# The clip of the new q and the seeds of stage 0: one VectorE operation over two PSUM banks in place of two

## The reference, cut to what matters

```python
def _derivative(q, p, drive, coupling, bias):
    i_couple = jnp.tanh(q) @ coupling.T
    dq = q - q ** 3 / 3.0 - p + drive + i_couple + bias
    dp = EPSILON * (q + ALPHA - BETA * p)
...
q_next = q + DT / 6.0 * (dq1 + 2 * dq2 + 2 * dq3 + dq4)
q_next = jnp.clip(q_next, -CLAMP, CLAMP)
```

## Time and profile before

| | |
|---|---|
| median of 3 runs | 619.08 us (618.81 to 619.54) |
| profiled execution, its own time | 620.08 us |
| its span | 618.2 us |
| granted TensorE clock, mean | 0.997 |
| PE busy | 582.3 us, 94% |
| DVE busy | 518.4 us, 84% |
| ACT busy | 407.9 us, 66% |
| POOL busy | 255.7 us, 41% |

### The profile page before, as it was taken

One profiled execution on the slowest core, in us unless ns is written; L12 is line 12 of the kernel. 1 busy time (PEld: TensorE's weight loads), 2 busy tenths in 40 slices (PEclk: granted clock), 3 DMA queues, 4 the chain that ended last, 5 costly groups with the idle time before them and its releaser, 6 DMA issues.

```text
span 618.2 us, 14209 instructions
## 1 busy us (share of the span) xinstructions
PE 582.3 (94%) x4918; PEld 525.3 (85%) x4918; DVE 518.4 (84%) x1544; ACT 407.9 (66%) x968; POOL 255.7 (41%) x401
## 2 busy tenths in 40 slices
PE   8899999999999889988888999999999999999997
PEld 7899999999999878877776887887887888888875
DVE  3777777777777768888988999999999999999996
ACT  2544454545454465567447888888888889888885
POOL 0333333332322453420154455565565565565550
PEclk9999999999999999989999999999999999999999
DMA  8400000000000000500000000000000000000001
GB/s 270 165 2 2 1 1 2 1 1 2 1 1 1 19 1 1 185 1 1 2 0 2 10 14 15 19 19 10 19 19 10 20 18 10 19 19 10 19 19 34
DMA packets 12517, 14.87 MB, mean 24 GB/s; under 512 B 1632, under 2 KB 10144, under 8 KB 12448
## 3 DMA queue, kind: packets, MB, share of 16 engines
q1 hardware_dynamic: 12448, 13.97, 6.7%
HBM read 9.78 MB, written 4.19 MB: 23 GB/s over the span
## 4 chain that ended last, share of the span: by engine, by line
PE 63%; DVE 16%; ACT 14%; issue 4%; SPq 1%; DMA 1%; POOL 0%; ACTq 0%; DVEq 0%
PE PS L451 18%; PE PS L313 16%; PE PS L336 12%; ACT q_s L761 4%; PE PS L505 3%; PE PS L527 3%; ACT k_s L740 2%; PE PS L489 2%; PE PS L372 2%; PE PS L429 2%; ACT big L672 2%; PE PS L389 2%; ACT q_s L801 2%; DVE h_s L1059 1%; DVE big L941 1%
## 5 line engine op out<-in xcount | busy, mean ns | idle before, releaser
L451 PE MATMUL PS<-k_s,h_s 128*128 128x128 f32 x1024 | 163.4, 287 | 4.7 <-DVE PS L1039 2.1
L451 PEld LDWEIGHTS PS<-k_s,h_s 128*128 128x128 f32 x1024 | 131.6, 191 | 24.7 <-DVE PS L1047 9.5
L313 PE MATMUL PS<-part 128*128 128x256 f32 x900 | 115.6, 286 | 0.6 <-issue 0.6
L313 PEld LDWEIGHTS PS<-part 128*128 128x128 f32 x900 | 109.8, 191 | 0.8 <-issue 0.8
L740 ACT ACTIVATE k_s<-h_s 128x128 f32<-128x128 f32 x256 | 71.3, 305 | 32.6 <-DVE h_s L1059 25.3
L336 PE MATMUL PS<-big,wrk 128*128 128x128 f32 x744 | 88.4, 275 | 3.0 <-DVE big L898 3.0
L336 PEld LDWEIGHTS PS<-big,wrk 128*128 128x128 f32 x744 | 85.8, 192 | 3.6 <-DVE big L898 3.6
L1207 POOL COPY h_s<-big 128x256 f32<-128x256 f32 x32 | 21.5, 671 | 130.8 <-DVE big L898 130.8
L451 PE MATMUL PS<-h_s 128*128 128x128 f32 x384 | 74.2, 275 | 0.0
L451 PEld LDWEIGHTS PS<-h_s 128*128 128x128 f32 x384 | 58.3, 192 | 0.0
L637 ACT ACTIVATE big<-big 128x256 f32<-128x256 f32 x32 | 13.3, 417 | 65.5 <-DVE big L880 65.5
(11 more groups left out here) (184 smaller groups left out, 1269.1 us busy)
## 6 DMA issues: line engine op xcount, KB each, us to landing
out<-q_s SPq DMA_DIRECT2D x32, 128.0 KB, 1.7
x_s<-in_xT SPq DMA_DIRECT2D x14, 256.0 KB, 5.9
k_s<-in_wgT SPq DMA_DIRECT2D x1, 832.0 KB, 6.1
k_s<-in_wuT SPq DMA_DIRECT2D x1, 832.0 KB, 7.8
k_s<-in_wih SPq DMA_DIRECT2D x3, 256.0 KB, 4.0
wrk<-in_whh SPq DMA_DIRECT2D x3, 256.0 KB, 4.4
h_s<-in_wdT SPq DMA_DIRECT2D x1, 768.0 KB, 7.8
x_s<-in_xT SPq DMA_DIRECT2D x4, 128.0 KB, 3.6
```

The costliest lines, as they stand in the source:

```text
L313: r = pe.matmul(p, y, x, start=i == 0, stop=i == len(passes) - 1)
L451: return pe.matmul(PS[:, m, 0:128], w, x, start=False, stop=True, skip_group_check=True)
```

## The change

Two pairs of DVE operations, each pair one operation per PSUM bank, become one operation each over both banks: the clip of the new q at the end of a step, and the seeds of stage 0 at the start of one. The semaphores are raised by two at once, and the waits become that for the second half.

```diff
                 ve.wait_ge(s_dr, drive_done(t))
-                for m in range(2):
-                    if t:
-                        ve.wait_ge(s_next, 8 * t - 1 + m)
-                    ve.tensor_tensor(PS[:, m, 0:128], I_at(t)[:, m], cm(pn[t % 2], m), ALU.subtract).then_inc(s_seed, 1)
+                if t:
+                    ve.wait_ge(s_next, 8 * t)
+                ve.tensor_tensor(PS[:, 0:2, 0:128], I_at(t), two(pn[t % 2]), ALU.subtract).then_inc(s_seed, 2)
...
                 nexts(4 * t + 3, lambda m: PS[:, m, 128:256])
-                for m in range(2):
-                    ve.wait_ge(s_next, 8 * t + 7 + m)
-                    ve.tensor_scalar(cm(qn[(t + 1) % 2], m), PS[:, m, 128:256], CLAMP, -CLAMP, ALU.min,
-                                     ALU.max).then_inc(s_q, 1)
+                ve.wait_ge(s_next, 8 * t + 8)
+                ve.tensor_scalar(two(qn[(t + 1) % 2]), PS[:, 0:2, 128:256], CLAMP, -CLAMP, ALU.min, ALU.max).then_inc(s_q, 2)
```

## The result

The changed kernel takes 624.41 us (median of 6 runs, 623.69 to 625.39), the kernel before 619.09 us (6 runs). The ratio is 1.0083, interval 1.0071 to 1.0095: slower by 0.8%. The forecast was 622.1 with a range up to 623.9, so the direction held and the size did not.

The account below looks back on a forecast made before the run. The ACT and DVE loops, both 9.17 a step, were taken to bound the kernel. 26 x 0.10 = 2.6 plus step 1, step 3 and tail gave 3.0, so 622.1 us, range 620.4 to 623.9.

Parts of the forecast that it names:

- The clip's wait: DVE at the step boundary: joint clip starts 0.03 behind the second new q's end, at 0.12 in place of 0.
- The clip's duration: DVE, joint clip over two banks: 0.42, with bounds of 0.289 and 0.683.
- Much slower: Rival, chance 0.05: an operation across two banks pays the fixed part twice, clip 0.56, time 626.0.
- Both loops equally long: ACT loop and DVE loop both take the 9.17 of one step; whichever grows sets the new period.
- The size per step: First tanh on ACT, then L761, L489 and the stage 1 matmul, each 0.10 later; period 9.27 for 9.17.
- The saving on DVE: Joined clips and seeds save 0.07 each, 0.14 against the new wait's 0.12; product moves from 0.79 to 0.78.
- The seeds: Stage 0 start: joining saves DVE 0.07; both seeds ready at 0.87, PE's first matmul 0.10 late but hidden.
- The places that hide or repeat the cost: Two stalled steps hide the delay; step 1 costs 0.25, step 2 0, step 3 0.05, the tail some 0.1.
- Free wait: Rival, chance 0.11: joint clip is short or starts at once, ACT loop stays 9.17, time 619.1.
- DVE alone sets the pace: Rival "faster", chance 0.05: the wait costs nothing and DVE saves 0.14 a step, 4.3 in all, time 614.8.

Follow-up runs that it names:

- split clips: Kernel before, but both clips, still one per bank, wait for the second new q: 623.61 us with that wait carried, 627.17 with it apart.
- clip from SBUF: Changed kernel, but the unclipped new q is written to SBUF and the joint clip reads it there: 620.80 us, ratio 1.0019.
- raised by one: Changed kernel, but the joint clip raises its semaphore by one instead of two, so its wait is carried: 623.88 us, ratio 1.0068.

## Why the prediction was right or wrong

**The clip's wait: mis-sized, and the failed term.** The prediction took 0.03 behind the new q's end from the pair of cubic and reader, and so had the clip start at 0.33. It starts at 0.40. That reader carries its late wait. The joint clip doesn't, and pays 0.10. The two pairs of runs that differ only in the place of a late wait show 0.06 to 0.07, with the clip joined and split. I had read one row for "a wait on the operation right ahead" without asking which of its waits was the late one. The GRU part of the same trace had both kinds. L898 starts 0.45 behind L894 in the first two steps, where it has one wait, and 0.52 in the 30 later ones, where a second wait is written first:

```profile
17.03 0.42 DVE L894 TENSOR_TENSOR big<-big 128x256 f32<-128x256 f32 x1
17.48 0.42 DVE L898 TENSOR_TENSOR big<-big 128x256 f32<-128x256 f32 x1
...
153.66 0.42 DVE L894 TENSOR_TENSOR big<-big 128x256 f32<-128x256 f32 x1
154.18 0.43 DVE L898 TENSOR_TENSOR big<-big 128x256 f32<-128x256 f32 x1
```

The split clips started 0.12 to 0.13 later for a wait carried and 0.19 to 0.20 later for one apart, where the clip of the kernel before started 0.21 behind the new q. The statement of the Trainium skill ("VectorE: DVE Perf Modes", section "The DRAIN you can't avoid") that a semaphore costs nothing extra doesn't hold for such a wait here.

**The clip's duration: right.** 0.42 was taken; L1142 took 0.42, over two banks as the copy did from one. "Much slower", the fixed part paid twice, falls.

**Both loops equally long: wrong, by 0.04 to 0.05.** The prediction saw the matmul of stage 1 load just as L489's loads ended, and took that for what let it go. L489's loads and the matmul behind them lie 0.37 apart when nothing else holds the matmul (after, 460.88 to 461.25, ahead of the shown end of L489's loads at 461.29) and lay 0.41 apart before. ACT's loop thus had 0.04 to 0.05 to spare, and the chain of waits, which went through ACT, named the loop that was second by a hair. All runs fit: L761 later by 0.07, 0.14 and 0.21 (clip from SBUF, raised by one, the changed kernel) made steps longer by 0.03, 0.095 and 0.165, each 0.04 to 0.05 less. Where DVE's loop alone was lengthened, by 0.13 and 0.20, the step followed it in full.

**The size per step.** Forecast 0.10; measured 0.16. With the wait carried it was 0.095, the size I gave, but from a delay of 0.14 at L761 less that slack, not from 0.10 with none: errors that cancel by luck. The 0.14 has two small parts that the forecast lacked: the tanh came 0.12 later and not 0.10, and from the tanh to the Square it is 0.42 where the tanh waits for the joint clip and 0.40 before (why, no run tests). Over the whole kernel the forecast had +3.0; stage and tail of the changed kernel grew by 4.9, and with the wait carried by 3.5. The difference, 1.5, is less than 28 x 0.07 = 1.9, for the stalls on "issue" fell otherwise (step 2 took 10.46 with the wait carried, 10.20 in both other kernels).

**The saving on DVE: right that nothing is left of it.** The product came at 1.07 in place of 1.00: 0.19 was paid and 0.12 saved (clip to seed 0.34 in place of 0.39, seed to product 0.33 in place of 0.40), not the 0.14 forecast. But the cubic then waits for the Square, which now ends 0.21 later, so DVE's loop became 0.12 longer by itself (seed of stage 1 at 2.75 for 2.63); the forecast had it unchanged.

**The seeds: right.** Joined alone they moved nothing in the steady steps.

**The places that hide or repeat the cost: right in part.** Step 1 had 0.23 (0.25 forecast), but by luck: its tanh came 0.34 later (0.52 to 0.86), and 0.11 of that was made up on the way to the next boundary. Step 2 had none, step 3 had 0.12 (0.05), the tail 0.3 (0.1). Before, steps 14 and 31 had the two stalls that were to hide the delay (9.38 and 9.52). After, step 14 took 9.46, step 28 took 9.57 and step 31 had no stall, so they moved and changed in size, and hid part of the cost: steps 4 to 31 have 4.29, where 28 x 0.165 would be 4.6.

**The rivals.** "Free wait" fell with both of its conditions, a short clip or one that starts at once: the clip took 0.42 and waited. "DVE alone sets the pace" was nearer the truth about the kernel before than I allowed, yet not for its price: with the seeds joined DVE's loop did not shorten, since the product then met its own wait for PE.

## What to carry to other kernels

Joining two operations saves a start, and makes the first half wait for the second: price the wait at the instruction right ahead, by a row with the same kind of wait.
## What the runs showed of the hardware

- A wait that clears late costs 0.03 from the result's end to the next start on DVE when the operation carries it (split clips, 0.33) and 0.10 when it is an instruction of its own (0.40). On PE the step from ACT's L761 to L489's loads went from 0.11 to 0.05 by the same exchange. A wait already fulfilled costs nothing in either place that these rows show: the pair of split clips lasts 0.49 with the waits carried and with the waits apart, and only the first of the two has to wait.
- One DVE operation over two PSUM banks, 128 columns each, takes what 256 columns of one bank take in L1171: 0.42.
- The clip of 256 columns from SBUF to SBUF took 0.30, and the next operation started 0.21 behind it, against 0.42 and 0.34 from PSUM.
